# Gated rounds of a graph kernel: a group's sums ahead of the tile's gates on TensorE

## The reference

```python
def step(h, Wl):
    m = h @ Wl
    agg = jax.ops.segment_sum(m[src], dst, num_segments=n)
    gi = agg @ w_ih.T + b_ih
    gh = h @ w_hh.T + b_hh
    ir, iz, in_ = jnp.split(gi, 3, axis=-1)
    hr, hz, hn = jnp.split(gh, 3, axis=-1)
    r = jax.nn.sigmoid(ir + hr)
    z = jax.nn.sigmoid(iz + hz)
    ng = jnp.tanh(in_ + r * hn)
    h_new = (1.0 - z) * ng + z * h
    return (h_new, None)
h, _ = jax.lax.scan(step, h, W)
cat = jnp.concatenate([h, x], axis=-1)
y = jax.nn.relu(cat @ l0_w.T + l0_b)
y = jax.nn.relu(y @ l1_w.T + l1_b)
return y
```

## Time and profile before

| | us |
|---|---|
| Median of 3 runs | 12400.03 (12399.82 to 12401.75) |
| The profiled execution | 12392.67 |
| its span, first to last instruction | 12390.9 |
| TensorE busy | 6595.2 |
| VectorE busy | 5386.9 |
| GpSimd busy | 8034.1 |
| ScalarE busy | 2191.3 |

### The profile page before, as it was taken

One profiled execution on the slowest core, in us unless ns is written; L12 is line 12 of the kernel. 1 busy time (PEld: TensorE's weight loads), 2 busy tenths in 40 slices (PEclk: granted clock), 3 DMA queues, 4 the chain that ended last, 5 costly groups with the idle time before them and its releaser, 6 DMA issues. The chain is left out here.

```text
span 12390.9 us, 162478 instructions
## 1 busy us (share of the span) xinstructions
PE 6595.2 (53%) x41938; PEld 6038.7 (49%) x41939; DVE 5386.9 (43%) x13456; ACT 2191.3 (18%) x7110; POOL 8034.1 (65%) x8298
## 2 busy tenths in 40 slices
PE   0000000355444456666666666666666666668996
PEld 0000000234333346666666666666666666667885
DVE  8882000344444434444444444444444444445554
ACT  0000000011133311111111111111111122224553
POOL 4777777677677766665666566656665655546774
PEclk9999999866655568887888888888888888889998
DMA  1000000222322243333333333333333322232222
GB/s 57 2 2 2 7 7 7 66 76 77 77 58 58 59 86 93 92 91 85 94 92 92 83 98 91 91 82 99 92 92 79 87 75 75 75 61 57 60 59 48
DMA packets 442833, 831.41 MB, mean 67 GB/s; under 512 B 179731, under 2 KB 260596, under 8 KB 442061
## 3 DMA queue, kind: packets, MB, share of 16 engines
q0 software_dynamic: 329728, 718.19, 23.2%
q1 hardware_dynamic: 112967, 111.54, 3.0%
HBM read 740.57 MB, written 88.61 MB: 67 GB/s over the span
## 5 line engine op out<-in xcount | busy, mean ns | idle before, releaser
L593 POOL DMA_INDIRECT rows<-state_table,idx x4160 | 4022.4, 967 | 2653.0 <-issue 1424.6
L639 DVE TENSOR_TENSOR agg<-agg,l_prod 128x250 f32 (+2 forms) x5824 | 2213.8, 380 | 4781.5 <-PE l_prod L616 3184.6
L616 PE MATMUL l_prod<-onehot,rows 128*128 128x125 f32 x16640 | 2430.7, 310 | 121.5 <-DMA rows<-state_table,idx 70.5
L616 PEld LDWEIGHTS l_prod<-onehot,rows 128*128 128x128 f32 x16640 | 2362.7, 228 | 143.8 <-DVE agg L639 71.5
L613 PE MATMUL l_prod<-rows,onehot 128*125 128x130 f32 (+1 forms) x3328 | 760.0, 402 | 2506.6 <-DMA rows<-in_x_dram,idx 1889.9
L613 PEld LDWEIGHTS l_prod<-rows,onehot 128*125 128x125 f32 x3328 | 663.9, 296 | 2581.8 <-issue 2188.0
L279 POOL DMA_INDIRECT slots_table<-rec_stage,row_stage x784 | 825.9, 1053 | 382.0 <-issue 242.7
L1507 POOL DMA_INDIRECT l_gathered<-xcol_table,l_idx x832 | 794.0, 954 | 342.4 <-issue 233.0
L622 DVE TENSOR_TENSOR onehot<-iota_row,rec 128x500 f32<-128x500 f32 x1465 | 984.5, 672 | 15.0 <-PEq L104 15.0
L593 POOL DMA_INDIRECT rows<-rel_table,idx x832 | 794.4, 955 | 301.3 <-issue 251.6
L593 POOL DMA_INDIRECT rows<-in_x_dram,idx x832 | 804.1, 966 | 254.4 <-issue 253.4
(11 more groups left out here) (274 smaller groups left out, 8734.7 us busy)
## 6 DMA issues: line engine op xcount, KB each, us to landing
rows<-state_table,idx POOLq DMA_INDIRECT x4160
slots_table<-rec_stage,row_stage POOLq DMA_INDIRECT x1568, 2.1
rel_table<-l_relrow SPq DMA_DIRECT2D x50, 500.0 KB
state_table<-l_row SPq DMA_DIRECT2D x200, 125.0 KB
rows<-in_x_dram,idx POOLq DMA_INDIRECT x832
rows<-rel_table,idx POOLq DMA_INDIRECT x832
l_gathered<-xcol_table,l_idx POOLq DMA_INDIRECT x832
slots_table<-fill SPq DMA_DIRECT2D x8, 936.0 KB
```

The costliest lines, as they stand in the source:

```text
L593: pool.indirect_dma_start(out=K["rows"][:, r, 0:width], out_offset=None, in_=table, in_offset=bass.IndirectOffsetOnAxis(ap=K["idx"][:, r:r ...
L616: last = pe.matmul(p[:, s * SLOT:s * SLOT + LANES], K["rows"][:, r, s * D:(s + 1) * D], oh, start=True, stop=True)
L639: dve.tensor_tensor(into, into, of, ALU.add).then_inc(S.added, 1)
```

## The change

In both bodies of the gated rounds the call of `sum_half` moves from the end of a step to its start. So each group's sums now stand ahead of what TensorE does for the tile in the same step. Nothing else changes: the same instructions, operands, waits and increments, and the order on the other engines is as it was.

```diff
@@ -1208,6 +1208,8 @@
                     for b in range(2):
                         now, _ = columns_of_places(nc, pe, PE, K, turn, b)
                         for n in range(4):
+                            if turn.chunks():
+                                sum_half(pe, K, S, prod, turn, 4 * b + n, STATE, False)
                             if now is not None:
                                 gates(turn, n, b, now, rnd)
                             if n == 3 and now is not None:
@@ -1216,8 +1218,6 @@
                                     last = pe.transpose(trs[0:LANES, s * D:(s + 1) * D], new[:, s, 0:LANES],
                                                         K["ident"][:])
                                 last.then_inc(rows_ps_ok, 1)
-                            if turn.chunks():
-                                sum_half(pe, K, S, prod, turn, 4 * b + n, STATE, False)
                 turns(pe, rnd, body, rounds)
```

## The result

| | us |
|---|---|
| Median of the kernel before | 12400.89 (12399.82 to 12401.84, 4 runs) |
| Median of the changed kernel | 11231.59 (11226.41 to 11238.76, 4 runs) |
| Ratio | 0.9058, interval 0.9042 to 0.9073 |
| The profiled execution after, its span | 11230.72, 11229.0 |

The change takes 1169 us off. The forecast was 11176 us; the measured time lies 56 us above it and inside the range of 11050 to 11370.

A forecast was written before the change was run, and what follows sets the result against it. The prediction took TensorE's chain with VectorE inside as the bound in all five gated rounds. Savings of 732.8 and 491.4 us, together 1224.2, took 12392.7 to 11168.5 us profiled, 11176 as the median; range 11050 to 11370.

The forecast's parts named there:

- The bound before and after: Gated rounds: TensorE's chain with VectorE inside bounds before, GpSimd's gathers after, at 1.286 us each, 20.6 us a half-turn.
- G0's wait: TensorE's r and h gate matmuls wait 2.42 us for VectorE's additions each half-turn; zero left after the change.
- T's wait: TensorE's transposes wait 5.3 us for the new state; 2.3 us left at the high clock, 0.6 at the low.
- TensorE's chain of 15.8 to 18.9 us: TensorE's half-turn in rounds 1 to 4 after the change, waits for state included, under the gathers' 20.6 us.
- The ends of the rounds: Last gather to the next round's first: 24.7 us instead of 53.1; 32.2 us after the last round's last gather.
- 2.9 until S3 starts: At a round's end, TensorE's last group of sums starts 2.9 us after the last gather's start.
- The sum: Whole kernel: rounds 1 to 4 save 732.8 us, the last 491.4, together 1224.2; profiled execution 11168.5 us.
- The rule against it: Gathers starting inside VectorE's one-hot comparison run longer: up to 0.115 us more per gather, 11533 us; 0.029 was kept.
- One-hots holding most gathers back: Rival in the gated rounds: VectorE's comparisons lengthen gathers to near 1.37 us, 11350 to 11533 us in all; chance 0.08.
- TensorE staying the bound: Rival: TensorE's clock does not rise, above all in the last round; 11280 to 11480 us; chance 0.08.
- Slower, with TensorE at 1.2 GHz throughout: Rival: sums wait for gathers in small pieces, half-turns of 25.8 us against 24.3, some 12700 us; chance 0.02.
- No change, with T's wait back in another place: Rival: the transposes' wait returns elsewhere, for instance behind VectorE; could cost 1 or 2 us, not 7; chance 0.01.

The follow-up runs named there:

- e5_half: Changed kernel gathering only the first two chunks of each group in the gated rounds, on a chip where the kernel before takes 15786 us: 11810.5 us.
- e6c_extra: Changed kernel with the product of the n gate made three times instead of once: 11241.28 us, ratio 0.9062 to the kernel before.
- e8b_onehot: Changed kernel with a group's one-hots built by four `tensor_scalar` comparisons instead of one `tensor_tensor`: 11168.91 us, ratio 0.9002 to the kernel before.

## Why the prediction was right, and where not

**The bound before and after: right.** TensorE's chain set the pace, and the gathers set it now: GpSimd has 5.8 us of waits for indices in 900 and a gather every 1.28 us. The forecast of 1.286 from the first stretch of the second round was the best choice among 1.257, 1.286 and 1.372: measured are 1.281 (round 1), 1.280, 1.282, 1.284 and 1.297 (the last). The four rounds are 14.6 us shorter for it than forecast. The last one is 8.7 us longer: 115 of its 832 gathers take over 1.0 us, 84 to 98 in the others.

**G0's wait: right.** "I take zero left": it is not in the list of waits.

**T's wait: right in kind.** 2.3 us or 0.6 were forecast, depending on the clock; 0.5 is seen, since the sums ahead of T wait in its place. In `e5_half`, where they don't, 2.4 us remain, the forecast's value at the high clock.

**TensorE's chain of 15.8 to 18.9 us: right as a bound.** Less than 20.5 by `e6c_extra`, 18.2 by `e5_half`. The working had TensorE waiting for rows only, 1 to 4 us; two thirds of its waits are for additions and one-hots, 60.7 and 48.0 beside 59.3. They may follow from the late rows, since VectorE can add a group only once it is summed, and builds one-hots behind that. In `e5_half`, where no rows are late, the waits for one-hots are gone and 36.6 us of those for additions remain, so at least part of these has another cause. They cost nothing while the chain has slack.

**The ends of the rounds: wrong, and this is the miss.** The step that failed is "2.9 until S3 starts". It took the 2.92 us of the second group of a round for the last group, whose rows are all one row: 16.7 us. With the rows spread the totals come out, 8.7 us to G0 and 25.4 in all against 8.9 and 24.7, but the terms on the way to G0 only by luck: 3.7 until S3 starts, 2.0 for S3 and 3.0 from there to G0, where 2.9, 3.6 and 2.4 were forecast. VectorE still has the new state to make when S3 is done, and the additions wait behind it. Four ends came out at 154.5 us in place of 98.8, 55.7 more, and the last at 48.0 in place of 32.2, 15.8 more. The kernel before shows the sign of it in a row that the prediction didn't look for, its window from 5600 us to the last gather of round 1:

```profile
5600.00:5687.00 87.00, 56.25 (x60) 0.80 0.58 87
```

The DMA share is 0.58 at 87 GB/s, where the earlier trace rows has 0.37 at 106 and 0.34 at 91 over a whole round.

**The sum.** From the forecast for the profiled execution, 11168.5: gathers of rounds 1 to 4 -14.6, gathers of the last +8.7, four ends +55.7, the last end +15.8, the start of the rounds -2.9. That gives 11231.2; the profiled execution took 11230.7. The ends of the rounds alone were 71.5 us too short.

**The rule against it: right in kind, and rightly given a small share.** Of the 0.115 us a gather that it could add, the prediction kept 0.029; 1.281 less 1.257 is 0.024. A gather that meets the comparison is held up; here in the changed kernel a gather before VectorE's comparison, the comparison, and the gather that starts inside it:

```profile
5954.08 0.95 POOL L593 DMA_INDIRECT rows<-state_table,idx  x1 [0.30 <-issue]
...
5955.04 0.67 DVE L622 TENSOR_TENSOR onehot<-iota_row,rec 128x500 f32<-128x500 f32 x1
...
5955.34 1.20 POOL L593 DMA_INDIRECT rows<-state_table,idx  x1 [0.30 <-issue]
```

The comparison ends at 5955.71, 0.37 us after the gather's start, and the gather is 0.25 us longer than the 0.95 of the one before. In the earlier trace rows it ends 0.47 us after the start, and the gather is 0.35 us longer. In both the extra time is what is left of the comparison 0.12 us after the gather's start. In the changed kernel's whole trace none of the 1970 gathers that start while VectorE stands idle takes over 1.0 us, and none of the 1296 that start in the additions `agg<-agg,l_prod`, which read one of their two tensors from PSUM. But 104 of 105 that start in `l_dd<-l_dd,l_gz` do, so the comparison is not the only instruction that holds gathers up. 91 of 832 gathers in the first round take over 1.0 us, one in nine, where the rival had one in four; `e8b_onehot` shows that 79 us hang on the form of the comparison. The Trainium skill (SBUF — State Buffer, Who interferes with whom) says that an instruction of VectorE with two inputs in SBUF contends with a GpSimd instruction that reads SBUF; the traces agree, with 1.20 us for the gather above. Its inference that such an instruction does not hold up the making of descriptors is not settled by them: the gather reads its indices from SBUF too, and no run here tells that read from the making of descriptors.

**The rivals.** One-hots holding most gathers back: out, 1.28 and not 1.37 us a gather. TensorE staying the bound: out by `e6c_extra`. Slower, with TensorE at 1.2 GHz throughout: out, the granted clock is 0.82 to 0.91 in the rounds. No change, with T's wait back in another place: out, the waits in front of the sums stay under the gathers' pace.

## What to carry to other kernels

Where two edits both shorten a chain that has a second bound close beneath, cost them as a pair: each alone may reach the floor. When a consumer is moved close behind its producer, look at what its lead had hidden, at the ends of the loop above all, where padding runs through the same path; filler slots should name different rows. The fastest version that ran is the changed kernel with spread fillers, 0.8976 of the time before; the one-hots by `tensor_scalar` save 79 us on the changed kernel, and the two together were not run.

## What the runs showed of the hardware that was not expected

- Gathers whose 128 indices are all the same row are slow, and a run of them falls behind: at a round's end 16.7 us pass from the issue of the last to the sums that use it, against 3.7 with different rows, at a DMA share of 0.93 and 80 GB/s against 0.38 and 109.
- A gather can take longer on GpSimd where it starts inside an instruction of VectorE on two tensors in SBUF: 0.95 us undisturbed, over 1.0 in 340 of the 456 that start inside the comparison, and in the two cases shown longer by what was left of the comparison 0.12 us after the gather's start.
- More matmuls can be nearly free: 15% more records, 5% more busy time, with the granted clock at 0.92 in place of 0.83.
- Chips differ: the kernel before takes 12393 to 12408 us in three sets of runs, and 15559 and 15786 us on two other chips, where TensorE's matmuls start singly with gaps that nothing awaited explains.
